# Hidden products turned through DRAM, key pass without PE transposes, down-weight low halves on GpSimd

## The reference, cut to what matters

```
x = x + layernorm(rs * (softmax(mask(Q K^T / 8)) V) Wo)      # Q of layernorm(x), K and V of ctx
h = layernorm(x)
w, e = top_k(softmax(h @ gate.T), 8);  w = w / sum(w)
x = x + sum over the 8 of w * ((silu(h @ w_gate[e]) * (h @ w_up[e])) @ w_down[e])
```

## Time and profile before

| | us |
|---|---|
| median of 3 runs | 6712.06 (6709.46 to 6721.78) |
| the profiled execution: its time | 6714.65 |
| its span, first to last instruction | 6713.0 |
| projections | 0 to 413 |
| attention | 413 to 2100 |
| output and routing | 2100 to 2836 |
| experts | 2836 to 6713 |

### The profile page before, as it was taken

The page is one execution under the profiler, slowest core; times in us unless marked ns, Lnnn a source line. Parts: engine busy times, 40 slices in busy tenths (PEclk is TensorE's granted clock), DMA queues, the critical chain, the costliest instruction groups (busy, mean ns, idle before and its releaser), DMA issues.

```text
span 6713.0 us, 107844 instructions
## 1 busy us (share of the span) xinstructions
PE 6472.6 (96%) x32234; PEld 5731.1 (85%) x32235; DVE 3663.3 (55%) x4544; ACT 2923.7 (44%) x3606; POOL 2308.0 (34%) x2178
## 2 busy tenths in 40 slices
PE   9999999999999999699999999999999999999998
PEld 7888887887888788589989888899899999989987
DVE  4443324999999799744454454443533444444444
ACT  3321224888888655333343343332422333333333
POOL 1000000000000155544545454554444444545554
PEclk9999999999999999899999999999999999999999
DMA  8863555555555676456676676665655656666666
GB/s 258 232 196 143 155 146 144 127 128 127 128 132 130 174 173 171 110 152 160 163 212 162 164 188 160 163 164 111 186 111 111 139 137 164 146 155 164 161 158 149
DMA packets 873577, 1049.72 MB, mean 156 GB/s; under 512 B 440705, under 2 KB 670849, under 8 KB 873474
## 3 DMA queue, kind: packets, MB, share of 16 engines
q0 software_dynamic: 123984, 368.70, 24.0%
q1 hardware_dynamic: 593104, 382.50, 23.6%
q10 hardware_dynamic: 156386, 297.29, 13.2%
HBM read 725.85 MB, written 322.31 MB: 156 GB/s over the span
## 4 chain that ended last, share of the span: by engine, by line
PE 33%; DMA 8%; issue 6%; DVE 4%; POOL 3%; ACT 2%; ACTq 1%; SPq 0%; another core or an unknown queue 0%; POOLq 0%; DVEq 0%
DMA out<-moe_y,moe_rec_s 4%; PE moe_ps_gate L1374 4%; PE moe_ps_gate L1375 4%; PE moe_ps_gate L1376 4%; PE moe_ps_up L1376 4%; PE moe_ps_up L1374 4%; PE moe_ps_up L1375 4%; PE moe_ps_y L1363 3%; PE moe_ps_y L1362 3%; PE moe_ps_y L1361 3%; DMA moe_tokens<-h2st,moe_rows 3%; POOL moe_tokens L1325 2%; DVE moe_ps_turned L1477 1%; DVE moe_d_lo L1467 1%; DVE moe_gu_lo L1467 1%
## 5 line engine op out<-in xcount | busy, mean ns | idle before, releaser
L1325 POOL DMA_INDIRECT moe_tokens<-h2st,moe_rows x1156 | 1273.1, 1101 | 515.2 <-issue 265.7
L1374 PE MATMUL moe_ps_gate<-moe_gu_hi,moe_xT_hi 128*128 128x384 f32 x2288 | 811.3, 355 | 73.8 <-DVE moe_xT_lo L1471 53.9
L1414 ACT COPY moe_y<-moe_ps_y 128x1024 f32<-128x1024 f32 x287 | 291.2, 1015 | 1249.4 <-DMA out<-moe_y,moe_rec_s 1051.9
L1375 PE MATMUL moe_ps_gate<-moe_gu_lo,moe_xT_hi 128*128 128x384 f32 x2288 | 784.4, 343 | 0.0
L1376 PE MATMUL moe_ps_gate<-moe_gu_hi,moe_xT_lo 128*128 128x384 f32 x2288 | 783.4, 342 | 0.0
L1376 PE MATMUL moe_ps_up<-moe_gu_hi,moe_xT_lo 128*128 128x384 f32 x2288 | 764.3, 334 | 0.0
L1375 PE MATMUL moe_ps_up<-moe_gu_lo,moe_xT_hi 128*128 128x384 f32 x2288 | 764.2, 334 | 0.0
L1374 PE MATMUL moe_ps_up<-moe_gu_hi,moe_xT_hi 128*128 128x384 f32 x2288 | 764.2, 334 | 0.0
L1484 DVE SCALAR_TENSOR_TENSOR moe_hidden<-moe_silu,moe_rec_w,moe_ps_up 128x384 f32<-128x384 f32 x286 | 175.8, 615 | 1009.2 <-PE moe_ps_up L1376 694.4
L1361 PE MATMUL moe_ps_y<-moe_d_hi,moe_hT_hi 128*128 128x512 f32 x1722 | 673.5, 391 | 12.8 <-DVE moe_hT_lo L1491 10.3
L1363 PE MATMUL moe_ps_y<-moe_d_hi,moe_hT_lo 128*128 128x512 f32 x1722 | 677.1, 393 | 0.0
(11 more groups left out here) (202 smaller groups left out, 14047.6 us busy)
## 6 DMA issues: line engine op xcount, KB each, us to landing
first_raw<-in_w_gate ACTq DMA_DIRECT2D x63, 1536.0 KB, 7.7
first_raw<-in_w_up ACTq DMA_DIRECT2D x63, 1536.0 KB
moe_raw_d<-in_w_down ACTq DMA_DIRECT2D x63, 1536.0 KB
proj_a_raw<-in_ctxT POOLq DMA_DIRECT2D x64, 512.0 KB, 5.6
kst<-proj_o SPq DMA_DIRECT2D x256, 128.0 KB, 2.8
vst<-proj_o SPq DMA_DIRECT2D x64, 512.0 KB, 2.6
qst<-proj_o SPq DMA_DIRECT2D x256, 128.0 KB, 2.2
att_kt<-kst SPq DMA_DIRECT2D x64, 512.0 KB, 3.5
```

What stands on the lines that cost most here:

```text
L1325: nc.gpsimd.indirect_dma_start(out=tokens[:, g * (H // G):(g + 1) * (H // G)], out_offset=None, in_=h2_quarters, in_offset=bass.IndirectOf ...
L1374: nc.tensor.matmul(o[:, 0:I], xT_hi[:, c], gu_hi[:, b, k, c], start=(c == 0), stop=False)
L1375: nc.tensor.matmul(o[:, 0:I], xT_hi[:, c], gu_lo[:, b, k, c], start=False, stop=False)
```

## The change

1. Hidden tile. PE's three transposes go. SP stores hidden(t) (128x384) to a scratch tensor `hst` in DRAM, waits for it to land, and loads it back in four DMAs as `hidden_g`, in which each quarter of the features stands on 32 partitions. DVE then transposes 32x32 blocks from there to PSUM (`turn_hidden`); ACT and DVE make the halves as before. The down weights are loaded with their rows permuted to match, in four DMAs instead of one.
2. Down weights' low halves. The three subtractions of 128x1024 go from DVE to GpSimd (`down_low`), after the tiles of the expert before. PE waits for them (`d_lo_done`) where it waited for DVE's.
3. Orders. GpSimd does add(t-1) ahead of gather(t+3), and goes by experts. ACT makes silu(t+1) at the end of tile t. The gate and up weights are split in four pieces of 128x1536 instead of eight of 128x768, and spread between the other steps. ACT issues the load of the next expert's down weights at the start of the first tile, after a wait for `d_lo_done`, where it did so after the expert before.
4. Projections. The normalized tile is written with its feature groups reordered and stored to `xnst` (tokens on rows); for the query sweep it is loaded in four DMAs and DVE transposes 32x32 blocks, four instructions of 128x1024 a block. PE's 256 transposes and ACT's 32 copies go.

```diff
@@ projections_pass @@
-        xin, xn, xT = s.sb("xin", [P, 2, H]), s.sb("xn", [P, 2, H]), s.sb("xT", [P, 2, C, P])
+        rows = s.sb("rows", [P, 4, H])
+        xin, xn = rows[:, 0:2], rows[:, 2:4]
+        xg = rows[:].rearrange("p q n -> p (q n)").rearrange("p (g n) -> p g n", g=GROUPS)
...
+                def turn(p, t2, b, k):
+                    n = number(p, t2, b)
+                    dve.wait_ge(xg_in, 16 * (P // W) * (2 * t2 + b + 1))
+                    dve.wait_ge(a_lo_done, (n - 1) * PIECES + k + 1)
+                    columns_of_piece = slice(k * CP * W, (k + 1) * CP * W)
+                    nc.vector.transpose(a_raw[:, chunks(k)].rearrange("p c t -> p (c t)"), xg[:, :, columns_of_piece]).then_inc(turned_done, 1)
...
-                            for c in range(C):
-                                last = nc.tensor.transpose(tps[:, jb, c], xn[:, jb, c * P:(c + 1) * P], ident[:])
-                            last.then_inc(t_done, 1)
@@ experts_pass, SP @@
                 def tile(t, is_first=False):
                     sp.wait_ge(hidden_done, t + 2)
+                    sp.wait_ge(hidden_in, 16 * G * (t + 1))
                     sp.sem_inc(sp_passed, 1)
+                    sp.dma_start(hst[:, :], hidden[:]).then_inc(hidden_stored, 16)
                     record(rec_w, t + 1, rec_w_in)
+                    sp.wait_ge(hidden_stored, 16 * (t + 2))
+                    sp.wait_ge(hT_done, t + 1)
+                    sp.sem_inc(sp_passed, 1)
+                    for k in range(G):
+                        part = hst[:, k * (I // G):(k + 1) * (I // G)].rearrange("(g b) n -> b g n", b=W)
+                        sp.dma_start(hidden_g[k * W:(k + 1) * W], part).then_inc(hidden_in, 16)
                     if not is_first:
                         sp.wait_ge(added, 16 * t)
@@ GpSimd @@
+                def down_low(e, b):
+                    for c in range(CI):
+                        pool.wait_ge(w_hi_done, PIECES * e + GU + c + 1)
+                        pool.sem_inc(pool_passed, 1)
+                        nc.gpsimd.tensor_tensor(d_lo[:, b, c], raw_d[:, c], f32(d_hi[:, b, c]), ALU.subtract).then_inc(d_lo_done, 1)
...
-                with pool.Fori(0, last_tile + 1) as t:
+                def tile(t):
+                    add(t - 1)
                     gather(t + 3)
-                    add(t - 1)
+
+                def expert(e, b, has_next, has_second):
+                    expert_tiles(pool, e, tile, tile)
+                    if has_next:
+                        down_low(e + 1, 1 - b)
+                experts(pool, expert)
@@ PE @@
                     down(t - 1, b_before)
-                    pe.wait_ge(hidden_done, t + 2)
-                    for c in range(CI):
-                        last = nc.tensor.transpose(hT_ps[:, c], hidden[:, c * P:(c + 1) * P], ident[:])
-                    last.then_inc(hT_done, 1)
                     if e is not None:
-                        pe.wait_ge(w_lo_done, PIECES * e + PIECES)
+                        pe.wait_ge(d_lo_done, CI * e + CI)
@@ ACT @@
                 def load_down(e):
-                    act.wait_ge(w_lo_done, PIECES * (e - 1) + PIECES)
+                    act.wait_ge(d_lo_done, CI * (e - 1) + CI)
                     act.sem_inc(act_passed, 1)
-                    act.dma_start(raw_d[:], w_down[bass.ds(e, 1)].rearrange("o (c p) i -> p (o c) i", p=P)).then_inc(raw_in[2], 16)
+                    for s in range(G):
+                        act.dma_start(raw_d[s * W:(s + 1) * W], grouped(w_down[bass.ds(e, 1)], s)).then_inc(raw_in[2], 16)
...
+                def tile(t):
                     tokens_high(t + 1)
+                    output(t - 1)
+                    turned_high(t)
+                    gated(t + 1)
+
+                def first_tile(t, e, b, more, is_first):
+                    tokens_high(t + 1)
+                    load_down(e)
+                    split(e, b, 0, 2)
                     output(t - 1, is_first)
+                    split(e, b, 2, 3)
+                    turned_high(t)
+                    split(e, b, 3, GU)
+                    gated(t + 1)
                     if more:
-                        load_gate_up(e + 1)
+                        load_gate_up(e + 1, 0)
+                        load_gate_up(e + 1, 1)
@@ DVE @@
                     tokens_low(t + 1)
+                    if e is not None:
+                        split(e, b, 0, 1)
                     turn_tokens(t + 2)
                     if e is not None:
-                        split(e, b, 0, GU)
+                        split(e, b, 1, 2)
+                    turn_hidden(t)
+                    if e is not None:
+                        split(e, b, 2, 3)
                     dve.wait_ge(hT_hi_done, t + 1)
-                    nc.vector.tensor_tensor(hT_lo[:], hT_ps, f32(hT_hi[:]), ALU.subtract).then_inc(hT_lo_done, 1)
+                    nc.vector.tensor_tensor(by_group(hT_lo), hT_v, f32(by_group(hT_hi)), ALU.subtract).then_inc(hT_lo_done, 1)
+                    if e is not None:
+                        split(e, b, 3, GU)
```

## The result

The changed kernel takes 7719.91 us (median of 4 runs, 7717.08 to 7722.37), the kernel before 6711.95: a ratio of 1.1498, 95% interval 1.1479 to 1.1518. That is 1008 us slower. I forecast 788 slower and a range up to 7700, so the time lies 20 us outside it. The direction and the places were as forecast, the size was not.

The account below looks back on a forecast made before the run. PE, busy 96% of the span, was taken to set the pace. Lead to 2993, rounds of 4483 and tail of 48 made 7524, less 28 in the projections: span 7496, prediction 7500 us, range 7000 to 7700.

Parts of the forecast that it names:

- Step 1: PE without transposes: 12.44 us a tile by PE alone in the experts, 28 us saved in the key sweep.
- Step 2: New loop through SP and GpSimd inside an expert: 13.5 us a tile, longer than PE's 12.44 and today's 12.78.
- D: Time the down weights' low halves are ready: 23.1 us after s, the issue of the last tile's hidden store.
- Step 3: Down weights' low halves on GpSimd: 2.2 us a subtraction, PE stalls 7.5 us at each of 63 expert changes.
- Step 4: ACT, held by the low halves at an expert change: second tile's hidden product stored 14.2 us after they are ready.
- The rival that takes step 4 away: PE's stall for the halves stays, ACT's hold and load interference go: 8 us less in 56 rounds, 7050; chance 0.13.
- Step 5: Gate and up weight loads just ahead of the second tile's hidden store delay it: 3 us once an expert, between 0 and 6.
- One-tile experts: Rounds of experts with a single tile: 20 us each, six of them.
- Lead: From the first expert matmul at 2852.5 through the nine-tile first expert: first low halves ready at 2993.
- Tail: From the last time low halves are ready to the kernel's end: 48 us.

Follow-up runs that it names:

- e5: The kernel before with the changed kernel's new projections alone, experts as before: 6677.17 us, ratio 0.9951.
- e8: The changed kernel with low halves on DVE, gather ahead of add, and SP's record for the add ahead of the hidden loads; DRAM pass stays: 7193.1 us.
- e2: The changed kernel with GpSimd's gather(t+3) ahead of add(t-1) again: 7249.0 us.
- e3: The changed kernel with SP issuing the record for add(t-1) ahead of its wait for the stored hidden tile and the four hidden loads: 7338.8 us.
- e12: The changed kernel with each GpSimd subtraction over 32 of its 1024 columns, the rest of the low halves left out: 7608.3 us.
- e11: The changed kernel without the gate and up weight loads of every expert but the first: 7398.8 us.
- e1: The changed kernel with the down weights' low halves made by DVE again, behind an expert's last tile: 7625.1 us.
- e4: The changed kernel with ACT's load of the next down weights moved from the start of the first tile to its end: 7848.6 us.
- e6: The kernel before with the three low-half subtractions on GpSimd and the down weights' load waiting for them; hidden stays with PE: 6854.0 us.

## Why the prediction was too small

**Step 1** held: 28 us in the projections (32 in e5), and 12.44 us for PE alone is what e8 shows inside a long expert (12.47). Its figure of 75 us of matmuls beside each 5 us of transposes is wrong: a sweep of 348 us for 8 blocks is 44 us a block. That was cover enough.

**Step 2** held inside an expert: 13.60 against 13.5. Its terms by their means: store to loads 2.6 (2.5 forecast), loads 1.5 (1.8), to the record 1.0 (1.0), from there to the add 2.7 (2.8), add 1.62 (1.6), rows with their gap 0.35 (0.8), to the records of gather 1.4 (0.9), these 1.8 (1.8), to the next store 0.55 (0.3). The loop from an expert's last tile to the next expert is 2 us longer, but no round from D to D runs through it: the next D is counted from the last tile's store. e2 and e3 each shorten this chain and bring the tiles to 12.5, which shows that it set the pace.

**Step 3.** GpSimd's subtraction took 2344 ns against 2.2 us:

```profile
L1345 POOL TENSOR_TENSOR moe_d_lo<-moe_raw_d,moe_d_hi 128x1024 fp32r<-128x1024 f32 x192 | 443.9, 2344 | 1.5
```

The estimate from the Trainium skill (GPSIMD Engine Reference, 3.1 Elementwise) was 2.25 us; the trace is 4% above it. D came at s + 22.7 in experts of three and more tiles (23.1 forecast), and at s + 28.3 in those of two, where the slow store is the last tile's own. The stall was 10 us, 57 times, instead of 7.5, 63 times.

**Step 4**, D + 14.2, was 14.8, and e12 shows that it is no separate term: when D comes 6.4 us earlier, the second tile's product waits for other links, and the distance grows to 19.3. Which links was not tried apart. The rival that takes step 4 away assumed independence, and so did my range.

**Step 5 failed**: "I take 3 us". It was 5.0 (7.6 against 2.6), and e11, without the loads, gives 5.6 per change. The row that I had, a gather of 6.6 us behind such a load, pointed nearer to it than the middle that I took. At 5 the forecast is 112 us higher, 7612, inside the range. It is the largest single term of what was missing.

**One-tile experts**: 24.8 us a round instead of 20, 29 us in six. **Lead**: the first D is at 2991, 26 us later than 2993 less the 28 of step 1. The first store is 8 us late: gate and up take 10.5 us instead of 8.3 (granted clock 0.74 from 2825.25 to 2834), DVE's product ends at 2839.3, and SP issues records until 2840.7. The row before had shown most of this: there the first product begins 13.2 us after the first matmul. The eight loops behind it take 127 us instead of 108, the first two of them over 21 each. Tail 52 instead of 48. Forecast rounds are 193 us short in all: 29 from one-tile experts, the rest 2.9 us on average in 56 longer ones. Of a round of three or more tiles, D to the second store is 0.6 over, the second tile's loop with the slow store 2.5 (step 5 is 2.0 of it), each further tile 0.1, and from the last store to D 0.4 under. With lead and tail this is the whole 223 us between 7496 and the span.

**The range.** Its four upward ends, 90, 170, 130 and 60, give 240 as independent terms, that is 7740. The 7700 that was stated is tighter than its own terms, and the time lies between the two.

The four loads of the down weights I had priced as issue time, 2.1 us, and it is that: 70 to 80 us in 63 changes.

What each part costs depends on the order in which it is undone. From the changed kernel: PE's transposes -515, then gather first -33, then halves on DVE -343, one load -78, casts together -25. The other way: halves -95, then both orders -432, then PE's transposes -363. The parts are links of one chain from a hidden product to the next. Each hides part of the next one, so single removals under-read their share (e1, e12) or over-read it (e2). I had expected 490 for e1, 660 for e2 and 290 for e4 by treating them as terms of a sum; they gave 95, 471 and -129.

## What to carry to other kernels

A hop through DRAM costs more than its transfers: it must be priced with every weight load that can be in flight, and with what stands behind it on the in-order engine that waits for it. Where four edits lengthen one chain, price the chain with each of them absent before adding their terms. The new key pass, where the same trick has some 44 us of matmuls a block to hide behind, is worth keeping; in the experts it has some 8.

## What the runs showed of the hardware

- A 192 KB store issued 2 to 5 us after 1.5 MB loads on another queue held its waiter for 7.6 us instead of 2.6 (means; in the change shown, at a DMA share of 1.04 and 344 GB/s, against 0.52 and 109 in a quiet tile). Without the two loads it was 2.2 (e11).
- GpSimd's three subtractions are recorded with 6.93 us from start to end in the changed kernel, where DVE is mostly idle beside them, and mostly with 7.6 in e6 (mean 7.56), beside DVE's work:

```profile
3453.28 1.63 POOL L1341 DMA_INDIRECT out<-moe_y,moe_rec_s  x1 [0.50 <-issue]
3454.36 7.63 POOL L1333 TENSOR_TENSOR moe_d_lo<-moe_raw_d,moe_d_hi 128x1024 fp32r<-128x1024 f32 x3
```

That is no sign of the two engines holding each other up. In e6 the first subtraction's record begins 0.55 us inside that of the add, and from one subtraction's start to the next it is 2.35 us there and 2.30 in the changed kernel. The Trainium skill (SBUF — State Buffer, Who interferes with whom) has the two engines contend where DVE reads two SBUF inputs. Those beside the subtractions here read one input from PSUM, or have only one, in one-tile experts too, so no run shows that case.
- In the change of expert shown above PE stood idle for 11.1 us, and the stretch after it has a granted clock of 0.50, with gate matmuls 0.32 us apart instead of 0.17:

```profile
4938.00:4942.00 4.00, 3.99 (x13) 4.00 (x14) 0.91 (x1) 2.41 (x2) 0.00 (x0) 0.50 0.87 181
```

That is some 2 us of PE's time. It was not what the second tile's product waited for: the up matmuls end at 4948.7, and DVE is busy with low halves until 4949.8. Over the experts PE is busy for 3891 us instead of 3733, though it has 858 transposes less, at a granted clock of 0.89 instead of 0.98. No run takes the clock's share of the loss apart from that of the waits.
